# Message-passing layer of a GNN stack: ScalarE seeds four PSUM banks for each graph's first chunk, and TensorE adds onto the seed

## The chip, the core and the metric

The kernel runs on one core of one Trainium2 chip. The metric is the device time in microseconds of one execution, the median of three runs. The core has TensorE (PE, with a separate row for its weight loads, PEld), VectorE (DVE), ScalarE (ACT), GpSimd (POOL) and SyncE (SP). Each engine runs its own instruction list in order; they meet only at semaphores.

## The reference

Four GNN layers run over 128 graphs of 128 nodes with 64 features each; adj is 128x128x128. Only layer 0 is touched by the change. Cut to what matters:

```python
def _L0_gnn_ref(x, adj, W1, b1, W2, b2):          # x is relu(layernorm(x)) here
    F = x.shape[-1]
    mask = (adj > 0.0).astype(x.dtype)
    W1a, W1b = (W1[:F], W1[F:])
    xj_proj = x @ W1a
    diff = x[:, :, None, :] - x[:, None, :, :]
    h = jax.nn.relu(xj_proj[:, :, None, :] + diff @ W1b + b1)
    hm = jnp.einsum('bjkh,bjk->bjh', h, mask)
    deg = jnp.sum(mask, axis=-1)
    return hm @ W2 + deg[..., None] * b2
...
h = jnp.maximum(_layernorm(x, axis=-1), 0.0)
x = x + _L0_gnn_ref(h, adj, L0_gnn_W1, L0_gnn_b1, L0_gnn_W2, L0_gnn_b2)
```

For an edge from node j to node k the hidden vector is relu(A[j] - C[k]), 192 wide, where A = h(W1a + W1b) + b1 and C = h W1b. It is summed over the neighbours k of j. Layers 1 to 3 follow (three dense GCN products, a normalised layer, a tanh layer) and are the same before and after.

## The kernel before

The adjacency mask holds about 12% of the pairs, so layer 0 works on edges only. The neighbours of a node get ranks 0, 1, 2, ... and each rank is a slot. A **chunk** is up to seven slots of 128 nodes. For each slot a one-hot matrix picks, for every node j, row C[k] of the neighbour with that rank. Each graph has n - 1 **own chunks** of seven slots (n is counted on the chip; two own chunks in most graphs, three in some, 265 in all 128) and one **shared chunk** of five slots, in which nodes with many neighbours borrow rows of others.

The seven slots of an own chunk lie in four PSUM banks (table OWN): banks 0, 1 and 5 hold two slots each (384 columns), bank 6 one (192 columns). A and C are kept negated and split in two fp16 parts, ac_hi and ac_lo. `pe_chunk` fills one bank as follows: two matmuls with the identity as weights write -A (high, then low part) into all slots of the bank (line 524; the first has start=True), then each slot gets two matmuls with its one-hot matrix that add C (line 532). VectorE then takes the minimum with 0 and adds it into a sum in SBUF (line 722 for own chunks; lines 731 and 734 for the shared one), and that frees the bank (`s_free[k]`).

The work of **one graph b is one step** on every engine. Four graphs (q = 0 to 3) are a group; a loop iteration is two groups, eight graphs, and the loop is the hardware loop `Fori(1, NI - 1)` with 14 iterations, the first and the last two groups being written out. In a step the engines do, in program order:

- PE: at q = 0 the transposes of the next group's adjacency (lines 424, 427); the product that makes A and C of graph b + 2 (line 481, `pe_ac`); the own chunks in an inner loop; then `between`: the transposes of the summed result of graph b - 1 (lines 493 to 496), its update product for b - 2 (505, 506) and at each q a piece of the next group's ranking (433, 434, 442; 448; 454; 471 to 473); then the shared chunk.
- ACT: at q = 0 four copies of the transposes (571 to 576); at q = 1 seven copies of the ranks (588); two copies of `pe_ac`'s product, `ac` and `ac_hi` (622, 623); the start value of the sum for b + 1 (631, `act_init`); at q = 1 four normalisations (581); `act_sum` (637, 638); at q = 3 `act_host_ranks`, seven copies (603, 604, 607) that depend on PE's lines 471 to 473.
- DVE: the one-hot matrices of the next chunk (698), then the drains of the current one; between the own and the shared chunk the ranking arithmetic and the update of x (760).
- POOL: `ac_lo` (767), the host rows (775, 780), and the pairwise sums of the finished graph (789 to 793).

A ring of four chunks of one-hot matrices lies between DVE and PE. The result's transposes and `pe_ac`'s product use the same bank 2, so the transposes of graph b - 1 wait until `ac_hi` of graph b + 2 is copied:

```python
            if not (known(b) and b + 4 > B):
                pe.wait_ge(s_hi, b + 4)
```

(in `pe_transpose_sum`, called with b - 1.)

## Time and profile before

| what | value |
|---|---|
| median of 3 runs | 1949.1 us (1948.92 to 1950.03) |
| span of the profiled execution | 1947.1 us, 2.0 us less than the median |
| PE busy | 1728.4 us (89%) |
| PE weight loads | 1332.5 us (68%) |
| DVE busy | 1313.8 us (67%) |
| ACT busy | 974.0 us (50%) |
| POOL busy | 712.6 us (37%) |

The span runs from the first to the last instruction; the timed runs also hold what lies around it, here about 2.0 us. Layer 0 takes the span from about 40 to 1425 us. Busy time of PE is modelled for pipelined matmuls, so the distance between two starts says more about its pace than the length of one matmul.

### The profile page before, as it was taken

To read this page: it belongs to the slowest core of one execution; us is meant where nothing else is said; L and a number is where in the kernel's file an instruction comes from. 1 tells how busy PE (TensorE), PEld (TensorE's weight loads), DVE (VectorE), ACT (ScalarE), POOL (GpSimd) and SP (SyncE) were. 2 spreads that over 40 slices of the span, in tenths; PEclk is the share of its full clock that TensorE was granted. 3 is DMA by queue.
4 is the path that set the end of the run, shared out by engine and by line. 5 is a ranking of instruction groups with operands and counts; after the bars stand their busy time and mean duration, and the time that the engine had idled before them with its cause. 6 is when DMAs were issued, how large, how long until landed. Compare 5 with 4: busy or idle time off the path is not lost. (4 is left out here: it accounts for less than half of the span.)

```text
span 1947.1 us, 49676 instructions
## 1 busy us (share of the span) xinstructions
PE 1728.4 (89%) x13837; PEld 1332.5 (68%) x13838; DVE 1313.8 (67%) x3568; ACT 974.0 (50%) x2265; POOL 712.6 (37%) x866
## 2 busy tenths in 40 slices
PE   1899999999989999999999999999979998995399
PEld 0677676766767676676767676677769887970276
DVE  5687787767878776777878777688834444456633
ACT  2455444545544454554444455454245554744555
POOL 0444444544444454444545444454400000026400
PEclk9999999999999999999999999999989998997699
DMA  5000000000000000000000000000000000000012
GB/s 117 7 12 7 6 6 6 6 6 11 6 6 6 6 6 6 11 6 6 6 6 6 6 6 12 6 0 1 2 0 0 0 0 0 0 0 1 6 40 41
DMA packets 40222, 18.57 MB, mean 10 GB/s; under 512 B 18792, under 2 KB 40106, under 8 KB 40106
## 3 DMA queue, kind: packets, MB, share of 16 engines
q1 hardware_dynamic: 39574, 17.28, 3.7%
q14 instruction: 100, 0.82, 0.1%
q8 instruction: 16, 0.26, 0.1%
q10 hardware_dynamic: 532, 0.21, 0.1%
HBM read 13.29 MB, written 4.19 MB: 9 GB/s over the span
## 5 line engine op out<-in xcount | busy, mean ns | idle before, releaser
L532 PE MATMUL bank<-ac_hi,work 128*128 128x192 f16 x2495 | 535.6, 248 | 0.0
L532 PE MATMUL bank<-ac_lo,work 128*128 128x192 f16 x2495 | 535.5, 248 | 0.0
L722 DVE SCALAR_TENSOR_TENSOR acc<-bank,acc 128x384 f32<-128x384 f32 (+1 forms) x1060 | 467.9, 494 | 25.9 <-PE bank L532 20.0
L789 POOL TENSOR_TENSOR acc<-acc 128x384 f32<-128x384 f32 x256 | 267.5, 1065 | 593.4 <-DVE acc L734 593.4
L524 PE MATMUL bank<-ac_hi,ident 128*128 128x384 f16 (+1 forms) x1060 | 331.2, 312 | 81.2 <-DVE acc L722 58.6
L698 DVE TENSOR_SCALAR work<-work,slot_key 128x896 f16 (+2 forms) x393 | 264.8, 674 | 108.3 <-issue 105.6
L524 PE MATMUL bank<-ac_lo,ident 128*128 128x384 f16 (+1 forms) x1060 | 329.3, 311 | 0.0
L532 PEld LDWEIGHTS bank<-ac_lo,work 128*128 x2495 | 246.7, 99 | 70.7 <-issue 3.7
L532 PEld LDWEIGHTS bank<-ac_hi,work 128*128 x2495 | 246.4, 99 | 71.0 <-issue 3.7
L637 ACT ACTIVATE hmTa<-bank,unscale 128x128 f32<-128x128 f32 x128 | 47.1, 368 | 491.2 <-PE bank L496 491.2
L524 PEld LDWEIGHTS bank<-ac_hi,ident 128*128 128x128 f16 x1060 | 104.5, 99 | 153.6 <-DVE acc L722 85.5
L731 DVE TENSOR_SCALAR acc<-bank 128x384 f32<-128x384 f32 x256 | 132.1, 545 | 55.0 <-PE bank L532 54.1
L767 POOL TENSOR_TENSOR ac_lo<-ac,ac_hi 128x384 f16<-128x384 f32 x128 | 122.7, 959 | 68.1 <-ACT ac_hi L623 68.1
L622 ACT ACTIVATE ac<-bank 128x384 f32<-128x384 f32 x128 | 64.3, 502 | 135.9 <-PE bank L481 135.9
L588 ACT ACTIVATE work<-bank 128x512 f16<-128x512 f32 x224 | 113.1, 619 | 17.6 <-PE bank L434 17.6
L631 ACT ACTIVATE acc<-ac,neg_pad 128x768 f32<-128x768 f32 x128 | 121.8, 952 | 0.0
L1312 POOL MEMSET work<- 8x512 f32 x1 | 0.5, 515 | 316.1 <-POOLq L1104 316.1
L524 PE MATMUL bank<-ac_lo,host 128*128 128x384 f16 (+1 forms) x384 | 114.7, 299 | 0.0
L524 PE MATMUL bank<-ac_hi,host 128*128 128x384 f16 (+1 forms) x384 | 114.7, 299 | 0.0
L481 PE MATMUL bank<-wac,hT 65*128 65x384 f32 x256 | 109.4, 510 | 3.5 <-ACT ac_hi L623 3.5
L524 PEld LDWEIGHTS bank<-ac_lo,ident 128*128 128x128 f16 x1060 | 105.3, 99 | 9.3 <-issue 7.0
L968 ACT ACTIVATE hn<-x_all,nmr,rstd 128x64 f32 (+1 forms) x256 | 91.2, 430 | 27.9 <-PE bank L1122 26.5
(204 smaller groups left out, 3330.5 us busy)
## 6 DMA issues: line engine op xcount, KB each, us to landing
adj_in<-in_adj_dram SPq DMA_DIRECT2D x32, 256.0 KB, 2.9
out_dram<-acc SPq DMA_DIRECT2D x32, 128.0 KB, 2.0
l1w<-in_L_gnn_W_dram SPq DMA_DIRECT2D x2, 64.0 KB
l1b<-in_L_gnn_b_dram SPq DMA_DIRECT2D x2, 64.0 KB
x_all<-in_x_dram SPq DMA_DIRECT2D x4, 0.2 KB, 11.8
nm_in<-in_nodemask_dram ACTq DMA_DIRECT2D x1, 64.0 KB
w1a<-in_L_gnn_W_dram ACTq DMA_DIRECT2D x1, 48.0 KB
w1b<-in_L_gnn_W_dram ACTq DMA_DIRECT2D x1, 48.0 KB
```

Source lines behind the costliest of these rows:

```text
L481: nc.tensor.matmul(pAC[:, 0:2 * H], hT0[:, p, q * N:(q + 1) * N], wac[:, :], start=True, stop=True)\
L524: nc.tensor.matmul(ps[:, 0:slots * H].rearrange("p (t h) -> p t h", t=slots), node, part[:, q, 0:H].unsqueeze(1).broadcast_to([N, slots, H ...
L532: last = nc.tensor.matmul(ps[:, t * H:(t + 1) * H], hot, part[:, q, H:2 * H], start=False, stop=(e == 1 and t == slots - 1))
L588: last = nc.scalar.activation(rs[:, p, :, t, :], pA3[:, :].rearrange("p (q j) -> p q j", q=GS), ACT.Copy, bias=-float(t))
L622: nc.scalar.activation(ac32[:, q % 2, :], pAC[:, 0:2 * H], ACT.Copy)
L631: nc.scalar.activation(acc[:, q, :].rearrange("p (t h) -> p t h", t=4), ac32[:, q % 2, 0:H].unsqueeze(1).broadcast_to([N, 4, H]), ACT.Relu ...
L698: nc.vector.tensor_scalar(onehot[:, ds(at, slots * N)], ranks.rearrange("p t j -> p (t j)"), slot_key[:, ds(key, 1)], None, ALU.is_equal). ...
L722: nc.vector.scalar_tensor_tensor(out=sums, in0=bank[n_bank][:, 0:slots * H], scalar=0.0, in1=sums, op0=ALU.min, op1=ALU.add).then_inc(s_fr ...
L731: nc.vector.tensor_scalar(sums, ps, 0.0, None, ALU.min).then_inc(s_free[k], 1)
L767: nc.gpsimd.tensor_tensor(ac_lo[:, q, :], ac32[:, q % 2, :], ac_hi[:, q, :], ALU.subtract)\
L789: last = nc.gpsimd.tensor_tensor(t[:, 0:2 * H], t[:, 0:2 * H], t[:, 2 * H:4 * H], ALU.add)
L968: ins = nc.scalar.activation(hn[:, u, (q + 1) * F:(q + 2) * F], x[:, ds((b + q) * F, F)], ACT.Relu, bias=nmr[:, ds(b + q, 1)], scale=rstd[ ...
```

## The change

Each graph's first own chunk gets its -A from ScalarE. A new function `act_seed` writes the sum of both parts (ac32, in fp32) into the slots of the four banks with four ACTIVATE copies, in the order bank 5, 0, 1, 6; each waits for its own bank to be free and signals `s_seed[k]`. It stands at the very end of ACT's step b and seeds for graph b + 1. In PE's list the first own chunk is taken out of the inner loop; it waits for the seed of each bank and issues only the 14 one-hot matmuls, none with start=True. The eight identity matmuls of line 524 are gone from that chunk. The other own chunks and the shared chunk are as before. Once, at the start, four 512-column matmuls write all four banks with start=True (`pe_open_banks`), so that later matmuls add. `act_ac` gets one wait more. DVE and POOL keep their lists.

```diff
--- before.py
+++ after.py
@@ -398,6 +398,8 @@
         s_lo = sem("AC_low_part_made")
         s_acc0 = sem("sum_initialised")
         s_G = sem("onehot_chunk_made")
+        s_open = sem("slot_banks_written_once")
+        s_seed = [sem(f"bank{k}_seeded") for k, *_ in OWN]
         s_done = [sem(f"edges_in_bank{k}") for k, *_ in OWN]
         s_free = [sem(f"bank{k}_summed") for k, *_ in OWN]
         s_half = sem("neighbour_sums_paired")
@@ -511,7 +513,14 @@
             eng.reg_mul(pos, pos, CH)
             return eng.snap(pos, min_val=0, max_val=(RING - 1) * CH)
 
-        def pe_chunk(pe, q, banks, node, regs):
+        def pe_open_banks(pe):
+
+            pe.wait_ge(s_mask, 1)
+            for _, n_bank, *_ in OWN:
+                last = nc.tensor.matmul(bank[n_bank][:, :], ident16[:, :], mask[:, 0, :], start=True, stop=True)
+            last.then_inc(s_open, 1)
+
+        def pe_chunk(pe, q, banks, node, regs, seeded=None):
 
             cnt, prev, full_prev, pos = regs
             pe.reg_mov(prev, cnt)
@@ -519,25 +528,31 @@
             at = ring_place(pe, pos, prev)
             for k, n_bank, first, slots in banks:
                 ps = bank[n_bank]
-                pe.wait_ge(s_free[k], full_prev if k == 2 else prev)
-                for e, part in enumerate((ac_hi, ac_lo)):
-                    nc.tensor.matmul(ps[:, 0:slots * H].rearrange("p (t h) -> p t h", t=slots), node,
-                                     part[:, q, 0:H].unsqueeze(1).broadcast_to([N, slots, H]),
-                                     start=(e == 0), stop=False)
+                if seeded is not None:
+                    pe.wait_ge(s_seed[k], seeded + 1)
+                else:
+                    pe.wait_ge(s_free[k], full_prev if k == 2 else prev)
+                    for e, part in enumerate((ac_hi, ac_lo)):
+                        nc.tensor.matmul(ps[:, 0:slots * H].rearrange("p (t h) -> p t h", t=slots), node,
+                                         part[:, q, 0:H].unsqueeze(1).broadcast_to([N, slots, H]),
+                                         start=(e == 0), stop=False)
                 if k == 0:
                     pe.wait_ge(s_G, cnt)
                 for t in range(slots):
                     hot = onehot[:, ds(at + (first + t) * N, N)]
                     for e, part in enumerate((ac_hi, ac_lo)):
                         last = nc.tensor.matmul(ps[:, t * H:(t + 1) * H], hot, part[:, q, H:2 * H],
-                                                start=False, stop=(e == 1 and t == slots - 1))
+                                                start=False, stop=(e == 1 and t == slots - 1),
+                                                skip_group_check=seeded is not None)
                 last.then_inc(s_done[k], 1)
 
         def pe_slots(pe, b, g, u, q, regs, between):
             pe.wait_ge(s_lo, b + 1)
             pe.wait_ge(s_n, g + 1)
             n = pe.value_load(chunks[0:1, ds(b, 1)], min_val=MINC + 1, max_val=MAXC)
-            with pe.Fori(0, n - 1):
+            pe_chunk(pe, q, OWN, ident16[:, :], regs, b)
+            pe.reg_add(regs[2], regs[2], 1)
+            with pe.Fori(0, n - 2):
                 pe_chunk(pe, q, OWN, ident16[:, :], regs)
                 pe.reg_add(regs[2], regs[2], 1)
             between()
@@ -619,6 +634,7 @@
             if not (known(b) and b < 2):
                 act.wait_ge(s_lo, b - 1)
                 act.wait_ge(s_acc0, b - 1)
+                act.wait_ge(s_seed[3], b - 1)
             nc.scalar.activation(ac32[:, q % 2, :], pAC[:, 0:2 * H], ACT.Copy)
             nc.scalar.activation(ac_hi[:, q, :], pAC[:, 0:2 * H], ACT.Copy).then_inc(s_hi, 1)
 
@@ -631,6 +647,24 @@
             nc.scalar.activation(acc[:, q, :].rearrange("p (t h) -> p t h", t=4),
                                  ac32[:, q % 2, 0:H].unsqueeze(1).broadcast_to([N, 4, H]), ACT.Relu,
                                  scale=neg_pad[:, p, q:q + 1]).then_inc(s_acc0, 1)
+
+        def act_seed(act, b, q, regs):
+
+            total, full, n = regs
+            if known(b) and b == 0:
+                act.wait_ge(s_open, 1)
+            else:
+                act.reg_load(n, chunks[0:1, ds(b - 1, 1)])
+                act.reg_add(total, total, n)
+                act.reg_alu(n, n, 1, ALU.subtract)
+                act.reg_alu(n, n, MINC, ALU.max)
+                act.reg_add(full, full, n)
+            for k, n_bank, _, slots in (OWN[2], OWN[0], OWN[1], OWN[3]):
+                if not (known(b) and b == 0):
+                    act.wait_ge(s_free[k], full if k == 2 else total)
+                nc.scalar.activation(bank[n_bank][:, 0:slots * H].rearrange("p (t h) -> p t h", t=slots),
+                                     ac32[:, q % 2, 0:H].unsqueeze(1).broadcast_to([N, slots, H]), ACT.Copy)\
+                  .then_inc(s_seed[k], 1)
 
         def act_sum(act, b, p, q):
             act.wait_ge(s_T, b + 1)
@@ -807,6 +841,7 @@
                 pe.reg_mov(regs[2], 0)
                 pe_adj(pe, 0, 0, 0)
                 pe_rank(pe, 0, 0)
+                pe_open_banks(pe)
                 pe_degrees(pe, 0, 0)
                 pe_ac(pe, 0, 0, 0, 0)
                 pe_sum_rows(pe, 0)
@@ -849,6 +884,9 @@
 
             @block.scalar
             def _(act):
+                seeds = [act.alloc_register(f"act_{r}") for r in ("chunks", "own_chunks", "graph_chunks")]
+                act.reg_mov(seeds[0], 0)
+                act.reg_mov(seeds[1], 0)
                 act_h(act, 0)
                 act_adj(act, 0, 0)
                 act_h(act, 1)
@@ -857,6 +895,7 @@
                 act_ac(act, 0, 0)
                 act_ac(act, 1, 1)
                 act_init(act, 0, 0, 0, 0)
+                act_seed(act, 0, 0, seeds)
                 act_rank_nodes(act, 0)
                 act_host_ranks(act, 0, 0)
 
@@ -880,6 +919,8 @@
                         act_sum(act, b - 1, *group_of(b, g, u, q, 1)[1:])
                     if nxt is not None and q == 3:
                         act_host_ranks(act, nxt, p)
+                    if not (known(b) and b + 1 >= B):
+                        act_seed(act, b + 1, (q + 1) % GS, seeds)
 
                 all_iterations(act, step)
                 act_sum(act, B - 1, 1, 3)
```

**TensorE, from the product of line 481 to the first matmuls of a graph (before).** `bank0_summed` is DVE's release of bank 0:

```order
L481 MATMUL bank2<-wac,hT0 128x384 [waits AC_high_part_made,h_transpose_copied]
L539 TENSOR_LOAD chunks [waits slot_counts_ready,AC_low_part_made]
L539 ISA x2
L540 UNCONDITIONAL_BRANCH
L517 ISA
L510 REGISTER_ALU
L511 ISA
L524 MATMUL bank0<-ac_hi,ident16 128x384 [waits bank0_summed]
L524 MATMUL bank0<-ac_lo,ident16 128x384
L532 ISA [waits onehot_chunk_made]
L532 MATMUL bank0<-ac_hi,work 128x192
L532 MATMUL bank0<-ac_lo,work 128x192
```

The same place now (`bank0_seeded` is ScalarE's signal, line numbers are those of the changed kernel):

```order
L483 MATMUL bank2<-wac,hT0 128x384 [waits AC_high_part_made,h_transpose_copied]
L552 TENSOR_LOAD chunks [waits slot_counts_ready,AC_low_part_made]
L552 ISA x2
L526 ISA
L512 REGISTER_ALU
L513 ISA
L544 ISA [waits onehot_chunk_made,bank0_seeded]
L544 MATMUL bank0<-ac_hi,work 128x192
L544 MATMUL bank0<-ac_lo,work 128x192
L544 ISA
L544 MATMUL bank0<-ac_hi,work 128x192
L544 MATMUL bank0<-ac_lo,work 128x192
```

The pair of identity matmuls that waited for VectorE's release is gone, the register instruction ahead of the first one-hot matmul waits for the one-hot matrices and for the seed, and the entry of the inner loop (UNCONDITIONAL_BRANCH) has moved behind this chunk.

**ScalarE, from the end of a step with q = 3 to the next step (before).** `work` written from `ranks` are the slot ranks of `act_host_ranks`, `adjT_all` is the first copy of the next step:

```order
L603 ACTIVATE ranks2<-bank3 128x512 [waits host_ranks_made]
L604 ACTIVATE work<-bank4 128x512
L607 ACTIVATE work<-ranks2 128x4x128 [waits host_ranks_copied]
L607 ACTIVATE work<-ranks2 128x4x128 x4
L571 ACTIVATE adjT_all<-bank3 128x512 [waits adj_transposed]
```

Now:

```order
L618 ACTIVATE ranks2<-bank3 128x512 [waits host_ranks_made]
L619 ACTIVATE work<-bank4 128x512
L622 ACTIVATE work<-ranks2 128x4x128 [waits host_ranks_copied]
L622 ACTIVATE work<-ranks2 128x4x128 x4
L657 TENSOR_LOAD chunks
L658 ISA
L665 ACTIVATE bank5<-ac32 128x384 [waits bank2_summed]
L665 ACTIVATE bank0<-ac32 128x384 [waits bank0_summed]
L665 ACTIVATE bank1<-ac32 128x384 [waits bank1_summed]
L665 ACTIVATE bank6<-ac32 128x192 [waits bank3_summed]
L586 ACTIVATE adjT_all<-bank3 128x512 [waits adj_transposed]
```

The four writes into the banks, with a load of the chunk count ahead of them, now stand between the host ranks and the next step's first copy.

**ScalarE, from the end of a step with q = 0 to the next step (before).** `work<-bank` is the rank copy of line 588, which waits for TensorE's ranks:

```order
L631 ACTIVATE acc<-ac32,neg_pad 128x768 [waits neighbour_sum_ready,AC_high_part_made,slot_counts_ready]
L637 ACTIVATE hmTa<-bank2,unscale 128x128 [waits sum_transposed]
L638 ACTIVATE hmTb<-bank2,unscale 64x128
L588 ACTIVATE work<-bank3 128x4x128 [waits ranks_made]
L588 ACTIVATE work<-bank3 128x4x128 x6
L622 ACTIVATE ac32<-bank2 128x384 [waits sum_initialised,AC_low_part_made,AC_product_made]
```

Now:

```order
L671 ACTIVATE hmTa<-bank2,unscale 128x128 [waits sum_transposed]
L672 ACTIVATE hmTb<-bank2,unscale 64x128
L657 TENSOR_LOAD chunks
L658 ISA
L665 ACTIVATE bank5<-ac32 128x384 [waits bank2_summed]
L665 ACTIVATE bank0<-ac32 128x384 [waits bank0_summed]
L665 ACTIVATE bank1<-ac32 128x384 [waits bank1_summed]
L665 ACTIVATE bank6<-ac32 128x192 [waits bank3_summed]
L603 ACTIVATE work<-bank3 128x4x128 [waits ranks_made]
L603 ACTIVATE work<-bank3 128x4x128 x6
L638 ACTIVATE ac32<-bank2 128x384 [waits sum_initialised,bank3_seeded,AC_low_part_made,AC_product_made]
```

The seven rank copies stand behind four writes, each of which waits for VectorE to free a bank.

## Rows read from the trace of the kernel before

**Rows 1.** The page: busy time of each engine.

```profile
PE 1728.4 (89%) x13837; PEld 1332.5 (68%) x13838; DVE 1313.8 (67%) x3568; ACT 974.0 (50%) x2265; POOL 712.6 (37%) x866
```

**Rows 2.** The page, costliest groups: identity matmuls (first part), and the drains.

```profile
L722 DVE SCALAR_TENSOR_TENSOR acc<-bank,acc 128x384 f32<-128x384 f32 (+1 forms) x1060 | 467.9, 494 | 25.9 <-PE bank L532 20.0
...
L524 PE MATMUL bank<-ac_hi,ident 128*128 128x384 f16 (+1 forms) x1060 | 331.2, 312 | 81.2 <-DVE acc L722 58.6
```

**Rows 3.** Waits in 100:1380: total us, times, longest.

```profile
PE bank L524 <- DVE acc L722: 57.6, 73, 3.0
...
PE bank L524 <- DVE acc L731: 20.3, 30, 0.9
```

**Rows 4.** Timeline of PE at a q = 1 graph: start, us, line, operation.

```profile
618.00 0.33 PE L524 MATMUL bank<-ac_hi,ident 128*128 128x384 f16 x1
...
618.33 0.24 PE L532 MATMUL bank<-ac_hi,work 128*128 128x192 f16 x1
...
618.65 0.33 PE L524 MATMUL bank<-ac_hi,ident 128*128 128x384 f16 x1
...
620.66 0.34 PE L524 MATMUL bank<-ac_hi,ident 128*128 128x384 f16 x1 [0.20 <-DVE acc L722]
...
622.97 0.41 PE L493 MATMUL bank<-ident,hm 128*128 128x128 f32 x2
```

**Rows 5.** Timeline of DVE, same stretch.

```profile
617.25 1.00 DVE L731 TENSOR_SCALAR acc<-bank 128x384 f32<-128x384 f32 x2
618.36 0.36 DVE L734 SCALAR_TENSOR_TENSOR acc<-bank,acc 128x192 f32<-128x192 f32 x1
619.02 1.12 DVE L698 TENSOR_SCALAR work<-work,slot_key 128x896 f16 x1 [0.30 <-issue]
620.06 1.74 DVE L722 SCALAR_TENSOR_TENSOR acc<-bank,acc 128x384 f32<-128x384 f32 x4
```

**Rows 6.** Timeline of ACT, same stretch.

```profile
615.68 3.54 ACT L588 ACTIVATE work<-bank 128x512 f16<-128x512 f32 x7 [0.49 <-PE bank L434]
619.04 0.56 ACT L622 ACTIVATE ac<-bank 128x384 f32<-128x384 f32 x1
619.41 0.57 ACT L623 ACTIVATE ac_hi<-bank 128x384 f16<-128x384 f32 x1
```

**Rows 7.** Timeline of PE at the q = 0 graph before it.

```profile
608.72 0.33 PE L524 MATMUL bank<-ac_hi,ident 128*128 128x384 f16 x1
...
611.01 0.33 PE L524 MATMUL bank<-ac_hi,ident 128*128 128x384 f16 x1
...
613.31 0.41 PE L493 MATMUL bank<-ident,hm 128*128 128x128 f32 x2
```

**Rows 8.** Timeline of DVE, same stretch.

```profile
609.58 1.87 DVE L722 SCALAR_TENSOR_TENSOR acc<-bank,acc 128x384 f32<-128x384 f32 x3
```

**Rows 9.** Timeline of ACT, same stretch.

```profile
606.88 2.71 ACT L607 ACTIVATE work<-ranks 128x512 f16<-128x512 f16 x5
609.49 0.57 ACT L571 ACTIVATE adjT_all<-bank 128x512 f32 x1
...
611.97 0.47 ACT L623 ACTIVATE ac_hi<-bank 128x384 f16<-128x384 f32 x1
```

**Rows 10.** Timeline of DVE behind a loop turn (q = 0).

```profile
653.10 0.72 DVE L698 TENSOR_SCALAR work<-work,slot_key 128x896 f16 x1 [4.87 <-issue]
```

**Rows 11.** Timeline of PE behind the same loop turn.

```profile
654.35 0.34 PE L524 MATMUL bank<-ac_hi,ident 128*128 128x384 f16 x1 [3.02 <-DVE acc L722]
```

**Rows 12.** Windows behind two other loop turns; PEclk is the granted clock.

```profile
569.20:573.20 4.00, 3.93 (x22) 2.94 (x23) 2.71 (x8) 0.00 (x0) 0.00 (x0) 0.57 0.00 0
994.50:998.50 4.00, 3.99 (x35) 3.31 (x35) 3.55 (x9) 0.43 (x2) 0.00 (x0) 1.00 0.00 0
```

**Rows 13.** Timeline of PE at the first graph.

```profile
62.83 0.53 PE L524 MATMUL bank<-ac_hi,ident 128*128 128x384 f16 x1
...
65.84 0.33 PE L524 MATMUL bank<-ac_hi,ident 128*128 128x384 f16 x1
```

## The prediction

> **What bounds the kernel now.** I read the busy shares first: TensorE leads with 89%, VectorE and ScalarE have 67% and 50% [rows 1]. That invites the sum "TensorE is the bound, so what it no longer does is gained". The groups and the waits speak against it. Of all matmul groups only the identity matmuls are preceded by idle time to speak of, 81.2 us over the run, mostly behind VectorE's drains [rows 2]. Within layer 0 TensorE stood 73 times at a bank that line 722 had yet to drain and 30 times at one that line 731 had [rows 3]. So TensorE and VectorE hand each other the banks, and the place where they meet is the start of a graph. There I read the timelines of single graphs.
>
> At a q = 1 graph TensorE starts the first own chunk at 618.00 and could start the second one 2.30 us later, at 620.30, but starts at 620.66 [rows 4]: VectorE first ends the shared chunk of the graph before (618.72), builds the next one-hot matrices, and starts its drains at 620.06 [rows 5]; the first drained bank releases TensorE. I call this start C2. At q = 2 and q = 3 the two starts lie more than 2.30 us apart as well, in nearly all groups. At a q = 0 graph it is 2.29 us [rows 7]: there TensorE sets the pace. The 13 turns of the hardware loop are an exception: VectorE idles 4.87 us for nothing but its own issue [rows 10] and TensorE 3.02 us behind it [rows 11]. So C2 belongs to VectorE in every graph except the 18 q = 0 graphs that follow no loop turn (31 changes of group less 13 turns) and the very first.
>
> **What is removed.** Of a two-slot bank the identity pair takes 0.33 us from start to start, the four one-hot matmuls 0.32 us [rows 4]. Three such pairs and a half-size one are 1.15 us per graph, 147 us over 128 graphs. Where C2 waits for VectorE this buys no time: the one-hot matmuls of bank 0 were already done over 1 us ahead of the first drain (618.65 against 620.06), and VectorE's order, its one-hot work and its drains are not touched. The saved time becomes a longer wait before C2. The bank that TensorE needs is the cover; I cost these removals at zero in 109 of 128 graphs.
>
> The Trainium skill, in Perfetto Trace Analysis, section Identifying the Most-Contended Engine, says that busy matmul time is a poor measure of TensorE's headroom and points to the busy share of the weight loads instead. The trace agrees: that share is 68% [rows 1]. By it TensorE has room left; the 89% alone would promise the 147 us.
>
> **What is added on ScalarE.** Four writes per graph. No row shows a ScalarE write into PSUM. The nearest is the copy of 384 elements out of PSUM: 0.37 us from start to start [rows 6], 0.47 us long [rows 9]. Seven 512-column copies take 3.36 us to the next start, 0.48 each [rows 6], so 128 columns more are 0.11 us, and 192 columns should step on by 0.21 us. One graph's seeds then take 3 x 0.37 + 0.21 = 1.32 us. Bounds: 0.8 us (two copies and a bit, should writes to PSUM be much quicker) and 2.3 us (0.57 us each without overlap, the longest copy in rows 6). I take the nearest row, 1.32. ScalarE has the time, 128 x 1.32 = 169 us in a half-idle engine; what matters is where it stands.
>
> The skill's ScalarE: Activation LUTs, section What ACT_TABLE_LOAD costs, gives 186 ns plus 0.833 ns per element with 93 ns of overlap between neighbours, which makes an estimate of 0.41 us per step and 1.49 us per graph. By that estimate each late place below would cost 0.1 to 0.2 us more.
>
> **Place one: q = 3 to q = 0, 18 times.** The seeds stand behind the seven host-rank copies. ScalarE comes free at 609.49 [rows 9]. Bank 5 is seeded from there, bank 0 from 609.86 to 610.33. TensorE, ready at 608.72, starts bank 0 at about 610.43 instead of 609.05. Before, VectorE's drain began 0.53 us after that start (609.58, [rows 8]), so now 610.96; one drain (1.87 / 3 = 0.62) and 0.05 to notice give C2 = 611.63 against 611.01 [rows 7]. That is +0.6 us, where an early seed would have gained. The delay runs on: C2, transposes, shared chunk, VectorE's ranking work and the next drains follow one another. 18 x 0.6 = +10.8 us. Bounds 0.2 us (quick writes) and 1.5 us (1 us more of writes): 4 and 27 us. At the loop turns TensorE waits until 654.35 anyway [rows 11], and seeds done near 651 are covered: nothing.
>
> **Place two: q = 0 to q = 1, 31 times.** Here the seeds are not late for the matmuls, since VectorE drains only at 620.06. But they hold up what is queued behind them on ScalarE: seven rank copies and the `ac`/`ac_hi` pair. Bank 0 is free at about 617.77, bank 1 at 618.25, bank 6 at 618.72 [rows 5]. Seeds: 617.84, 618.31, 618.79; the rank copies can start at 619.0 instead of 615.68. `ac_hi` ended at 619.98 [rows 6]; it now ends 3.3 us later, at 623.3. The transposes of line 493 wait for it, since they use its bank, and would start at 622.97 [rows 4]; with some 0.1 us to notice that is +0.4 us. The next step's whole chain hangs on them. 31 x 0.4 = +12.4 us. Bounds 0 (ScalarE's copies 10% quicker) and 1.0 us (seeds one after the other without overlap): 0 and 31 us.
>
> At q = 0 itself `ac_hi` ended 0.87 us ahead of the transposes (612.44 against 613.31, [rows 7, 9]). It comes 1.32 us later and the transposes 0.6 us later: just in time, I count nothing; each further 0.1 us on ScalarE would cost 18 x 0.1. At q = 2 and q = 3 nothing long stands between the seeds and `ac_hi`, which comes at most 3 us later and had more than that to spare: nothing.
>
> **The rest.** The four opening matmuls lie at the start beside ScalarE's rank copies: nothing. The first graph's first chunk ran at the low clock, 3.01 us for 2.30 [rows 13], with its seeds long there: -1.5 us. Moving the inner loop's entry behind the first chunk costs nothing where TensorE waits for VectorE; at place one it has about 0.3 us to hide in.
>
> **The clock.** Behind a loop turn the granted clock is 0.57 in one window and 1.00 in another [rows 12]; of the 13 turns ten have such a dip. 0.57 over 4 us means 3.4 us at the lower of the two levels (1.2 instead of 2.4 GHz), 1.7 us of lost work. Before each turn's wait TensorE will now be less busy, so the three spared turns may dip too: up to +5 us, I take +2.5. The skill's TensorE: Matmul & The Clock Gate, section What's actually happening, says that activity is what releases the throttle; by that, sparser first chunks can only add dips.
>
> **Sum.** 10.8 + 12.4 - 1.5 + 2.5 = +24.2 us on a span of 1947.1 gives 1971.3; with the 2.0 us around it, which also separate the span from the median 1949.1, 1973.3 us: slower by 1.2%.
>
> **Rivals.**
> *TensorE bound after all.* If its work set the pace at most starts, some of the 147 us would come back. For it: 89% busy. Against it: the waits at C2. What it can really claim is the 18 q = 0 starts, where C2 could move from 611.01 to VectorE's first release near 610.2, 0.8 x 18 = 14 us, with place two free: about 1934. It needs ScalarE to seed in time there, against its order.
> *Everything covered.* ScalarE's writes are so quick or the delays so absorbed by waits of others that both places come to under 0.1 us: 1949. Against it: at both places the slack is smaller than the delay, by rows.
> *The clock falls in ordinary steps.* With 1.15 us less work around each start, TensorE is half idle for some 3 us. If that drops the clock behind the 18 late starts as it does behind loop turns, 18 x 1.7 = 31 us more: 2004. Against it: three turns with 3 us of idleness kept 1.00. This mechanism decides once it strikes more than a handful of starts.
> *ScalarE is slower at it than its copies.* At the upper bounds of both places, with register load and waits in its queue: +27 + 31 + about 18 x 0.5 for the transposes at q = 0: 2015.
>
> **Chances.** Forecast (1958 to 1990) 0.63, slower-ScalarE 0.10, clock 0.09, covered 0.10, TensorE bound 0.08. A run tells no change from one of 0.2%, about 4 us. Faster 0.09, same 0.10, slower 0.81. The range takes in the lower bounds of the two places and most of the two slower cases: 1953 to 2002; the forecast's own range is 1958 to 1990.
>
> **What would show it.** Right: TensorE's busy time lower by about 140 us at a longer span; a wait of 1.2 to 1.6 us at C2 for q = 1 to 3; a wait of ScalarE's seed at q = 0; a short idle time before the transposes at q = 1, ended by the copy of `ac_hi`. Wrong: C2 at q = 0 earlier than before relative to the shared chunk, seeds that take under 0.8 or over 2 us, or a granted clock below 1.00 away from the loop turns.

## The result and the profile after

| what | before | after |
|---|---|---|
| median of the runs | 1949.0 us (1948.5 to 1950.0, 4 runs) | 2006.4 us (2005.2 to 2006.8, 4 runs) |
| span of the profiled execution | 1947.1 us | 2003.6 us |
| mean granted clock | 0.966 | 0.943 |

The change makes the kernel 2.9% slower: the ratio is 1.0294, 95% interval 1.0279 to 1.0308. The forecast was 1973.3 us, its range 1953 to 2002; the sign was right and the size less than half of what was measured (24 of 57 us).

The page after, first its busy times and the clock in 40 slices, then three groups (columns: line, engine, operation, out<-in, shapes, count | busy us, mean ns | idle time before, releaser). L536 are the identity matmuls, L544 the one-hot ones, L665 the seeds:

```profile
PE 1655.7 (83%) x12817; PEld 1240.5 (62%) x12818; DVE 1313.2 (66%) x3568; ACT 1175.3 (59%) x2778; POOL 710.8 (35%) x866
...
PEclk9899998999999999989999999989989999998599
...
L544 PE MATMUL bank<-ac_hi,work 128*128 128x192 f16 x2495 | 532.3, 255 | 109.8 <-ACT bank L665 109.5
...
L665 ACT ACTIVATE bank<-ac 128x384 f32<-128x384 f32 (+1 forms) x512 | 218.4, 449 | 186.7 <-DVE acc L765 185.6
L536 PE MATMUL bank<-ac_hi,ident 128*128 128x384 f16 (+1 forms) x548 | 183.4, 335 | 94.7 <-DVE acc L756 94.1
```

TensorE has 73 us less work than in [rows 1], VectorE the same, ScalarE 201 us more, and the whole is 57 us longer. The idle time ahead of the identity matmuls was 81 us [rows 2] and is now 95 us, and a new one of 110 us stands ahead of the one-hot matmuls. The clock row shows an 8 in four slices of layer 0 where it held a 9 before.

The waits of 100 to 1430 us (columns: who waited for whom, us in total, times, longest) give the new pattern; they answer to [rows 3]:

```profile
ACT bank L665 <- DVE acc L765: 178.3, 90, 2.4
...
PE bank L544 <- ACT bank L665: 105.5, 120, 1.6
...
PE bank L536 <- DVE acc L756: 89.7, 104, 2.1
...
DVE acc L756 <- PE bank L544: 54.8, 67, 1.8
...
PE bank L495 <- ACT ac_hi L639: 6.7, 30, 0.3
```

TensorE waits for a seed 120 times, in nearly every graph of this stretch, and VectorE now waits 55 us for TensorE's first bank. The last row is place two of the prediction, 30 times.

**Place one (q = 0).** The graph of [rows 7 to 9] lies 23.52 us later here (its product for graph b + 2 starts at 631.59, before at 608.07). ScalarE:

```profile
630.39 2.71 ACT L622 ACTIVATE work<-ranks 128x512 f16<-128x512 f16 x5
633.00 1.55 ACT L665 ACTIVATE bank<-ac 128x384 f32<-128x384 f32 x4
634.50 0.58 ACT L586 ACTIVATE adjT_all<-bank 128x512 f32 x1
...
636.97 0.47 ACT L639 ACTIVATE ac_hi<-bank 128x384 f16<-128x384 f32 x1
```

TensorE and VectorE beside it:

```profile
634.03 0.25 PE L544 MATMUL bank<-ac_hi,work 128*128 128x192 f16 x1 [1.64 <-ACT bank L665]
...
635.20 0.25 PE L544 MATMUL bank<-ac_lo,work 128*128 128x192 f16 x1
635.49 0.33 PE L536 MATMUL bank<-ac_hi,ident 128*128 128x384 f16 x1
...
637.79 0.41 PE L495 MATMUL bank<-ident,hm 128*128 128x128 f32 x2
```

```profile
634.57 1.75 DVE L756 SCALAR_TENSOR_TENSOR acc<-bank,acc 128x384 f32<-128x384 f32 x4 [1.55 <-PE bank L544]
```

The seeds take 1.50 us to the next start (633.00 to 634.50), not 1.32. TensorE's first matmul starts 0.08 us from where it was forecast (634.03 - 23.52 = 610.51, forecast 610.43), but the second chunk starts at 635.49 - 23.52 = 611.97: 0.96 us later than the 611.01 of [rows 7], not 0.6. VectorE's drain is not what it waits for (there is no wait in that row). Its own way there is longer: 1.17 us from the first to the last of the 14 matmuls (13 steps of 0.08 us would be 1.05; the rest is the wait for the next seed), and then 0.29 us until the inner loop's first matmul starts, where the step within a chunk is 0.08. The weight load there stands behind 0.27 us of its own issue:

```profile
635.48 0.10 PEld L536 LDWEIGHTS bank<-ac_hi,ident 128*128 128x128 f16 x1 [0.27 <-issue]
```

**Place two (q = 1).** Shifted by 24.47 us against [rows 4 to 6] (product at 641.80, before at 617.33):

```profile
642.31 1.26 ACT L665 ACTIVATE bank<-ac 128x384 f32<-128x384 f32 x3 [2.19 <-DVE acc L765]
643.50 3.51 ACT L603 ACTIVATE work<-bank 128x512 f16<-128x512 f32 x7
...
647.21 0.57 ACT L639 ACTIVATE ac_hi<-bank 128x384 f16<-128x384 f32 x1
```

```profile
645.14 0.34 PE L536 MATMUL bank<-ac_hi,ident 128*128 128x384 f16 x1 [0.73 <-DVE acc L756]
...
647.83 0.49 PE L495 MATMUL bank<-ident,hm 128*128 128x128 f32 x2 [0.22 <-ACT ac_hi L639]
```

C2 stands where it did, within 0.02 us (645.14 - 24.47 = 620.67, against 620.66 in [rows 4]): here VectorE sets it, as forecast. `ac_hi` ends at 647.78, which is the forecast's 623.3 + 24.5, and the transposes wait for it and start 0.39 us later than in [rows 4].

**The clock.** The surprise stands at ordinary starts. Two q = 2 graphs with the same work, C2 to the transposes, as windows (columns: window, length, busy us and instructions of PE, PEld, DVE, ACT and POOL, granted clock, DMA share, GB/s):

```profile
475.70:479.70 4.00, 4.00 (x23) 2.94 (x24) 2.91 (x7) 0.75 (x1) 2.42 (x4) 0.57 0.00 0
566.70:570.70 4.00, 3.99 (x36) 3.31 (x37) 3.77 (x9) 1.19 (x3) 2.44 (x4) 1.00 0.00 0
```

In the first, TensorE gets mostly the lower of its levels (1.2 GHz) and does 23 matmuls where the second does 36. Its timeline ahead of the drop shows two waits in the 3.7 us before C2: 1.45 us for the seed, then the 14 one-hot matmuls of the first chunk, then 0.74 us at C2. The clock falls within the first identity matmuls:

```profile
473.49 0.25 PE L544 MATMUL bank<-ac_hi,work 128*128 128x192 f16 x1 [1.45 <-ACT bank L665]
...
474.71 0.25 PE L544 MATMUL bank<-ac_lo,work 128*128 128x192 f16 x1
475.69 0.45 PE L536 MATMUL bank<-ac_hi,ident 128*128 128x384 f16 x1 [0.74 <-DVE acc L756]
475.94 0.53 PE L536 MATMUL bank<-ac_lo,ident 128*128 128x384 f16 x1
...
479.67 0.41 PE L495 MATMUL bank<-ident,hm 128*128 128x128 f32 x2
```

From C2 to the transposes it took 3.98 us there and 2.31 us in the other graph. Before the change no ordinary start looked like this: between 100 and 1380 us there were ten low stretches, all at loop turns. After it there are 24 in the same window: at all 13 loop turns, ten of them twice as long as before, and at 11 ordinary starts (a twelfth lies behind 1380 us).

The two waits of a start, added, tell which starts are struck. Medians from the two timelines, loop turns left out:

| starts | waits before | waits after | starts with a drop after |
|---|---|---|---|
| q = 0 | 0.0 us | 1.7 us | 6 of 18 |
| q = 1 | 0.2 us | 1.0 us | none |
| q = 2 | 0.9 us | 1.9 us | 6 of 32 |
| q = 3 | 0.1 us | 0.9 us | none |

The drops fall where TensorE now idles most, though not at every such start.

**Where the 57 us went.** I took each graph's distances between three fixed points (start of the shared chunk of the graph before to C2, C2 to the transposes, transposes to the start of the shared chunk) from both timelines and subtracted:

| starts | number | forecast | measured | of this the clock |
|---|---|---|---|---|
| first graph | 1 | -1.5 | -2.1 | 0 |
| q = 0 behind no turn (place one) | 18 | +10.8 | +28.0 | 8.5 (6 graphs) |
| q = 1 (place two) | 32 | +12.4 | +14.4 | 0 |
| q = 2 | 32 | 0 | +9.3 | 9.3 (6 graphs) |
| q = 3 | 32 | 0 | -0.1 | 0 |
| loop turns | 13 | +2.5 | +8.6 | 13.6 (all 13) |
| sum | | +24.2 | +58.1 | 31.4 |

The clock's share of a graph is its excess over full-clock neighbours of the same q; at the loop turns it is what the way from C2 on has grown. In place one 19.5 us are left without the clock, 0.97 us in most graphs and 2.9 in the last of the 18. Behind layer 0 the two traces part by less than 2 us (58.1 against 56.5 us of span).

At the loop turns C2 itself comes 5.0 us earlier in sum, 0.4 each, and 4.7 of them are VectorE's. Before, GpSimd made `ac_lo` beside the first one-hot work behind the turn; now `ac_hi`, and with it `ac_lo`, comes later, and that work runs alone. The turn of [rows 10], before and then after:

```profile
652.66 0.91 POOL L767 TENSOR_TENSOR ac_lo<-ac,ac_hi 128x384 f16<-128x384 f32 x1 [1.09 <-ACT ac_hi L623]
```

```profile
677.86 0.45 DVE L732 TENSOR_SCALAR work<-work,slot_key 128x896 f16 x1 [4.68 <-issue]
...
679.09 0.91 POOL L801 TENSOR_TENSOR ac_lo<-ac,ac_hi 128x384 f16<-128x384 f32 x1 [2.58 <-ACT ac_hi L639]
```

The same instruction takes 0.45 us instead of 0.72 [rows 10]. In the trace of the kernel before, the 100 of these instructions that no GpSimd work overlaps take 0.43 to 0.46 us each; the 151 that GpSimd overlaps for more than half of their length take 0.99 us on average. This is read from the traces; no run isolates it.

### The profile page after: what moved, and what is told of

Read it like the earlier page. It is cut to its first block and busy times, and to the rows that moved or that the text cites. A ratio compares the mean times of both kernels' runs of the same rounds, so it can differ in the third digit from the quotient of the medians.

```text
span 2003.6 us, 48629 instructions
## 1 busy us (share of the span) xinstructions
PE 1655.7 (83%) x12817; PEld 1240.5 (62%) x12818; DVE 1313.2 (66%) x3568; ACT 1175.3 (59%) x2778; POOL 710.8 (35%) x866
## 5 line engine op out<-in xcount | busy, mean ns | idle before, releaser
L544 PE MATMUL bank<-ac_hi,work 128*128 128x192 f16 x2495 | 532.3, 255 | 109.8 <-ACT bank L665 109.5
L544 PE MATMUL bank<-ac_lo,work 128*128 128x192 f16 x2495 | 530.3, 254 | 0.0
L544 PEld LDWEIGHTS bank<-ac_hi,work 128*128 x2495 | 251.5, 101 | 265.2 <-issue 216.1
L665 ACT ACTIVATE bank<-ac 128x384 f32<-128x384 f32 (+1 forms) x512 | 218.4, 449 | 186.7 <-DVE acc L765 185.6
L544 PEld LDWEIGHTS bank<-ac_lo,work 128*128 x2495 | 252.8, 101 | 51.2 <-issue 10.8
L536 PE MATMUL bank<-ac_hi,ident 128*128 128x384 f16 (+1 forms) x548 | 183.4, 335 | 94.7 <-DVE acc L756 94.1
L536 PE MATMUL bank<-ac_lo,ident 128*128 128x384 f16 (+1 forms) x548 | 181.9, 332 | 0.0
L536 PEld LDWEIGHTS bank<-ac_hi,ident 128*128 128x128 f16 x548 | 56.8, 104 | 123.3 <-DVE acc L756 119.2
L536 PE MATMUL bank<-ac_lo,host 128*128 128x384 f16 (+1 forms) x384 | 114.8, 299 | 0.0
L536 PE MATMUL bank<-ac_hi,host 128*128 128x384 f16 (+1 forms) x384 | 114.8, 299 | 0.0
L809 POOL TENSOR_SCALAR host<-row_f,start 128x128 f16<-128x128 f32 x128 | 76.5, 612 | 85.6 <-DVE shift L723 85.6
```

What stands on the lines that cost most here:

```text
L536: nc.tensor.matmul(ps[:, 0:slots * H].rearrange("p (t h) -> p t h", t=slots), node, part[:, q, 0:H].unsqueeze(1).broadcast_to([N, slots, H ...
L544: last = nc.tensor.matmul(ps[:, t * H:(t + 1) * H], hot, part[:, q, H:2 * H], start=False, stop=(e == 1 and t == slots - 1), skip_group_ch ...
L665: nc.scalar.activation(bank[n_bank][:, 0:slots * H].rearrange("p (t h) -> p t h", t=slots), ac32[:, q % 2, 0:H].unsqueeze(1).broadcast_to( ...
```

## Experiments

All were timed beside runs of the kernel before on one chip: 1949.6 us (7 runs) for the first four, 1949.5 us (17 runs) for the others.

### The clock alone: the change with filler matmuls

```diff
+        def pe_fill(pe, b, count):
+            pe.wait_ge(s_x0, b - 2)
+            for _ in range(count):
+                nc.tensor.matmul(bank[7][:, 128:512]..., ident16[:, :], before16[:, :]..., start=True, stop=True)
...
                         pe_ac(pe, b + 2, *group_of(b, g, u, q, -2))
+                    fills = 7
+                    if fills and not (known(b) and b < 3):
+                        pe_fill(pe, b, fills)
```

Seven matmuls of 384 columns, whose result nobody reads, stand ahead of the first own chunk in every step from the fourth graph on.

> The changed kernel, and in every step from the fourth graph on TensorE issues seven matmuls of 384 columns into unused columns of bank 7, behind pe_ac and ahead of the first own chunk (1.15 us of work, about what the change took away; their result is never read). Theory A (of the 57 us, some 32 are the two late places and some 27 are new or longer stretches at the lower clock, because TensorE is too little busy around the start of a graph): the new stretches go, the places stay: about 1980 us (1975 to 1986), granted clock near 0.965. Theory B (the lower clock has another cause, or costs nothing and the time is lost elsewhere): 2004 to 2008. Theory C (TensorE's own work bounds the steps): slower than the changed kernel, up to 2006 + 147.

Measured: 1983.7 us (1982.0 to 1986.6, 4 runs), ratio 1.0174 (1.0157 to 1.0191): inside the expected range and 23 us less than the changed kernel. The same table reads, from the slowest of the four runs: q = 0 +19.0, q = 1 +14.3, q = 2 +0.1, loop turns +5.8. More work on TensorE made the kernel faster; q = 2 costs nothing any more, and the rest at q = 0 is place one without the clock. The two waits of a start, added, are back at 0.2, 0.8 and 0.1 us for q = 1 to 3 and 0.6 us for q = 0, and outside the loop turns no low stretch is left. So the clock's part is shown, and its cause is what TensorE does around the start. The turns kept a cost, of another kind: what follows C2 is 13.3 us shorter than before the change, but C2 comes 19.1 us later.

```profile
314.18 0.25 PE L544 MATMUL bank<-ac_lo,work 128*128 128x192 f16 x1
317.45 1.11 PE L426 MATMUL bank<-ident,adj_in 128*128 128x128 f32 x4 [3.03 <-issue]
```

The waits of this kernel have it 8 times in 13 turns:

```profile
PE bank L426 <- issue: 26.1, 8, 3.7
```

There TensorE itself stands still at the turn of the hardware loop, which it does neither before nor after the change, nor in any other run. Why is open.

### ScalarE's queue alone: four copies more, TensorE as before

```diff
@@ before
+            act.wait_ge(s_seed[3], b)
+            for k, n_bank, _, slots in (OWN[2], OWN[0], OWN[1], OWN[3]):
+                act.wait_ge(s_free[k], full if k == 2 else total)
+                nc.scalar.activation(spare[k], ac32[:, q % 2, 0:H]..., ACT.Copy).then_inc(s_seed[k], 1)
```

The kernel before, with the four copies at the seeds' place and with their waits (and the wait added to `act_ac`), but written to spare SBUF that nobody reads.

> The kernel before, and ScalarE makes the four copies of -A with the same waits at the same place, but into spare SBUF that nobody reads; TensorE does all its identity matmuls as before. Theory A (ScalarE's queue pays at q = 0 to 1 and at the transposes of q = 0, and the clock loss needs TensorE's missing work): 31 x 0.46 = 14 us and 18 x 0.5 to 0.7 = 11 us, clock as before: 1973 us (1968 to 1979). Rival (ScalarE's time is free, and the whole loss comes from TensorE waiting for seeds): 1949. Rival (the copies themselves upset the clock or VectorE): above 1990.

Measured: 1967.7 us (1962.5 to 1968.9, 4 runs), ratio 1.0087 (1.0068 to 1.0107), just under the expected 1968 to 1979. q = 1 costs 14.4 us, as much as in the changed kernel, so place two is ScalarE's order and has nothing to do with PSUM or TensorE. At q = 0 C2 does not move (0.0 us), but C2 to the transposes grows by 0.6 us each, 11.1 us. The waits name the cause:

```profile
PE bank L495 <- ACT ac_hi L626: 15.2, 46, 0.6
```

So the forecast's "just in time" for `ac_hi` at q = 0 was not just in time; in the changed kernel this cost lies hidden under the larger delay of C2 (there `ac_hi` ends at 637.44 and the transposes start at 637.79). The turns became 9.1 us shorter, which the expectation lacked: C2 comes 5.3 us earlier, mostly by VectorE's quicker one-hot work, as in the changed kernel (0.45 us at each turn, without GpSimd beside it), and the low stretches from 100 to 1380 us are eight instead of ten. The four copies take 1.49 us from start to start here too, from SBUF to SBUF, so the seeds' step is not a matter of PSUM. The mean clock of 100 to 1380 us is 0.99 as before: without sparser first chunks it does not drop more.

### Place two mended: four rank copies ahead of the seeds

```diff
-                            act_rank(act, nxt, p)
+                            act_rank(act, nxt, p, 4)
...
+                    if nxt is not None and q == 0:
+                        act_rank(act, nxt, p, 0, 4)
                     if not (known(b) and b + 1 >= B):
                         act_seed(act, b + 1, (q + 1) % GS, seeds)
```

> The changed kernel with one order changed on ScalarE: four of the seven rank copies stand ahead of the seeds of the q = 0 step, three behind them in the q = 1 step. Theory A: ac_hi is early again, the 0.46 us per q = 1 step go (14.5 us), nothing else moves but a stretch or two of low clock: 1992 us (1987 to 1997). Rival (the delay at q = 1 would be absorbed by the waits that follow): 2006. If seeds for q = 1 come late now, C2 moves at q = 1 and it is over 2006.

Measured: 1988.0 us (4 runs), ratio 1.0172 (1.0125 to 1.0219), inside the expected range but with wide scatter: 1972.2 us at a mean clock of 0.958 up to 1999.1 us at 0.941. The profiled run was the slowest. In it q = 1 went from +14.4 to +0.8 us, which settles place two; q = 2 rose to +17 us, all clock (13 graphs with a drop instead of six), so in this profile more than half of the gain was given back. With such scatter one profile does not show that the new order causes the additional drops.

### Place one mended: five host-rank copies behind the seeds

```diff
+                    if nxt is not None and q == 3:
+                        act_host_slot_ranks(act, nxt, p)
```

> The changed kernel with the other order changed on ScalarE: the five slot-rank copies of act_host_ranks stand behind the seeds of the q = 3 step instead of ahead of them. Theory A: the seeds are in time at q = 0, C2 comes 0.97 us earlier than now and up to 0.6 us earlier than in the kernel before at the 18 starts: 18 to 27 us, and fewer stretches of low clock at q = 0 (up to six of 1.4 us): 1978 us (1970 to 1989). Rival (slot ranks late for VectorE at the next one-hot work take it back): 1995 or more.

Measured: 1998.2 us (1991.8 to 2006.6, 4 runs), ratio 1.024 (1.0217 to 1.0264): the expectation of 1978 failed, and the rival's 1995 came by another cause than the one it named. In the profile, again of the slowest run, at q = 0 C2 comes 0.93 us earlier than before the change, the gain that the rival "TensorE bound" promised, and nothing of it remains:

```profile
631.47 0.34 PE L536 MATMUL bank<-ac_hi,ident 128*128 128x384 f16 x1
...
635.42 0.49 PE L495 MATMUL bank<-ident,hm 128*128 128x128 f32 x2 [1.49 <-ACT ac_hi L641]
```

The transposes now wait 1.49 us for `ac_hi`, which ScalarE reaches only behind seeds, host ranks, adjacency copies and `ac`. Up to C2 the sum over the 18 graphs is -16.8 us, from C2 to the transposes +26.7 us. The transposes of a typical q = 0 graph come 0.68 us later than before the change, as with ScalarE's copies alone. The order of seeds and slot ranks does not matter for that: both stand ahead of `ac_hi` either way. Other orders were not tried, such as `ac` and `ac_hi` ahead of the four adjacency copies; before the change their product was computed at about 608.9 and copied from 611.60 on. The rest of the time is clock again (q = 2: +21.7 us).

### Both orders mended

```diff
+                        act_rank(act, nxt, p, 0, 4)
...
+                        act_host_slot_ranks(act, nxt, p)
```

> The changed kernel with both orders changed on ScalarE (rank copies 4 and 3 around the seeds, slot-rank copies behind the seeds), nothing filled. Theory A: nothing lost at q = 1; at q = 0 C2 comes 0.9 us early but the transposes then wait for ac_hi, whose queue is 1.4 us longer with 0.87 us to spare: +0.55 us times 18 = 10 us; the clock takes 25 to 35 us: 1985 us (1975 to 1998), scattered. Rival (the early C2 is kept): 1950 to 1965.

Measured: 1971.4 us (1964.3 to 1989.5, 4 runs), ratio 1.0101 (1.0074 to 1.0128), the median 4 us under the expected range. The profiled run, again the slowest, has q = 0 at -16.8 and +26.8, q = 1 at +0.8, q = 2 at +23.2 (clock). The four runs line up by the clock: spans 1962.6, 1962.6, 1976.9 and 1987.9 us at mean clocks 0.956, 0.956, 0.947 and 0.943. The same program and data, so the spread of 25 us goes with the clock, and such drops are partly chance. Profiled was the slowest run alone, so the split of the faster ones is not known.

### No seed at q = 0, rank copies split, with and without filler

```diff
-            pe_chunk(pe, q, OWN, ident16[:, :], regs, b)
-            pe.reg_add(regs[2], regs[2], 1)
-            with pe.Fori(0, n - 2):
+            if q > 0:
+                pe_chunk(pe, q, OWN, ident16[:, :], regs, 3 * g + q - 1)
+                pe.reg_add(regs[2], regs[2], 1)
+            with pe.Fori(0, n - 1 if q == 0 else n - 2):
...
+            if q == 0:                               # in act_seed
+                return
...
+                    fills = 7 if q > 0 else 0        # in the first of the two kernels only
+                    if fills and not (known(b) and b < 3):
+                        pe_fill(pe, b, fills)
```

ScalarE seeds only the graphs of q = 1 to 3, so that both causes of place one are gone, and place two is mended as above.

> The changed kernel with all three suspected costs taken out: no seed for graphs with q = 0 (TensorE starts these itself, as in the kernel before), four rank copies ahead of the seeds of the q = 0 step and three behind, and seven idle matmuls of 384 columns into unused columns of bank 7 at q = 1 to 3 (their result is never read). Three quarters of ScalarE's seeds are still made and still used. Theory A (two late places and the clock are the whole loss, and the removed work was worth nothing): the time of the kernel before, 1949 us (1945 to 1954), clock near 0.966. Rival (something else in the seeds costs, such as the wait for them at q = 1 to 3): 1960 or more. Rival (the removed work is worth something once the late places are gone): under 1943.

> The same as the kernel with all three taken out, but without the idle matmuls. Theory A: what is above the kernel before is the clock alone: one stretch of about 1.5 us at some q = 2 graphs and longer stretches at loop turns: 1965 us (1957 to 1982), scattered from run to run, clock 0.945 to 0.958. Rival (idleness of TensorE at q = 1 to 3 does not touch the clock): 1949.

Measured: with filler 1949.2 us (1947.7 to 1950.5, 11 runs), ratio 0.9998 (0.9989 to 1.0007); without 1956.7 us (1954.0 to 1961.6, 6 runs), ratio 1.0045 (1.0032 to 1.0057). The first came as expected, the second just under its range. With both places and the clock taken care of, the whole loss is back, so nothing else in the seeds costs time. That kernel cannot show what the removed matmuls are worth, since the filler puts as much work in their place. The one without filler can: 96 graphs have 1.15 us less of TensorE's work each, and at q = 1 to 3 the way to C2 is the same to 0.2 us in sum over 32 graphs, since VectorE sets C2 there. In its profile q = 2 is +15.5 us, all of it low clock (ten graphs with a drop), while the turns are 7.5 us shorter than before, with five low stretches from 100 to 1380 us instead of ten. So the sparser starts do not simply add drops: here they came at q = 2 and fewer were left at the turns. Why is open.

### The kernel before with filler at the loop turns

```diff
@@ before
                         pe_ac(pe, b + 2, *group_of(b, g, u, q, -2))
+                    fills = 16 if (q == 0 and u == 0 and not known(b)) else 0
+                    if fills and not (known(b) and b < 3):
+                        pe_fill(pe, b, fills)
```

> The kernel before, with 16 idle matmuls of 384 columns (2.6 us) ahead of the first chunk of the first graph behind each loop turn, where TensorE stood idle for 3.0 us (their result is never read). Theory A (the low clock behind loop turns comes from that idle time, and VectorE's late one-hot work hides the filling): the ten stretches go, 10 x 1.65 = 16 us: 1933 us (1930 to 1938), clock 0.975 or more. Rival (low clock has another cause there): 1949. Rival (TensorE's longer instruction list stalls it at the turn, or the filling is on the path): 1950 or more.

Measured: 1935.2 us (1934.3 to 1936.7, 5 runs), ratio 0.9926 (0.9913 to 0.9939), as expected. It beats both kernels, with 224 matmuls more than before. At the turn of the first window of [rows 12] it reads:

```profile
563.67 2.76 PE L540 MATMUL bank<-before,ident 128*128 128x384 f16 x16
...
569.15 0.34 PE L524 MATMUL bank<-ac_hi,ident 128*128 128x384 f16 x1 [0.42 <-DVE acc L729]
```

The windows behind this turn and behind that of [rows 11]:

```profile
569.10:573.10 4.00, 3.95 (x34) 3.27 (x35) 3.60 (x9) 0.39 (x2) 0.00 (x0) 1.00 0.00 0
652.50:656.50 4.00, 3.96 (x35) 3.29 (x35) 3.58 (x9) 0.41 (x2) 0.00 (x0) 1.00 0.00 0
```

VectorE still idles at each turn (103.8 us of issue in its one-hot line over layer 0, as before), and TensorE still waits for it, but the filler takes up most of the wait: 0.42 us at C2 are left of 3.02. The clock holds at 1.00 in both windows, and no low stretch is left from 100 to 1380 us. The turns are 16.3 us shorter in sum. One graph is 2.6 us longer, the first of the hardware loop: the filler stands there too, behind no turn and with no wait to fill.

The mean granted clock of 100 to 1380 us beside it, one row for each of four kernels: before, after, the change with filler, and this one.

```profile
100.00:1380.00 1280.00, 1195.34 (x10035) 907.80 (x10035) 975.95 (x2623) 640.98 (x1412) 606.74 (x752) 0.99 0.02 6
```

```profile
100.00:1380.00 1280.00, 1080.40 (x8680) 787.48 (x8681) 932.89 (x2518) 793.77 (x1811) 576.48 (x719) 0.95 0.02 6
```

```profile
100.00:1380.00 1280.00, 1183.82 (x9621) 867.87 (x9619) 939.58 (x2544) 809.32 (x1841) 587.37 (x730) 0.98 0.03 7
```

```profile
100.00:1380.00 1280.00, 1229.38 (x10379) 929.98 (x10377) 984.47 (x2651) 645.25 (x1422) 612.33 (x760) 1.00 0.02 6
```

The clock is lowest where TensorE's busy time is, and highest where that is (1195, 1080, 1184 and 1229 of 1280 us).

## Why the prediction was right and wrong

**What bounds the kernel: right.** C2 at q = 1 to 3 stayed where VectorE puts it, and the 147 us of removed work bought nothing. The kernel with q = 0 left alone and without filler shows it most plainly: 96 graphs seeded, C2 where it was, and 7 us more by the clock.

**Place two: right in mechanism and size.** +12.4 forecast, +14.4 measured (0.38 us at the transposes and 0.07 behind them, where 0.4 was forecast), reproduced by ScalarE's copies alone and removed by splitting the rank copies.

**Place one: the mechanism right, the term too small.** 0.6 us was forecast, 0.97 measured in most of the 18 graphs, together 19.5 us without the clock instead of 10.8. Two steps failed. The seeds' length was taken from copies out of PSUM (0.37 us from start to start); it is 0.41. The estimate from the Trainium skill's ScalarE: Activation LUTs, section What ACT_TABLE_LOAD costs, which the prediction kept beside its sum, was 1.49 us per graph, and the row shows 1.50: it was nearer than my nearest row. And I let VectorE's first drain set C2, at 611.63, with "about 0.3 us to hide in" for the inner loop's entry. There was nothing to hide in: the 14 one-hot matmuls alone, 1.15 us from the forecast start of 610.43, end at 611.58. Seeds that release TensorE bank by bank cost it 0.2 us more (0.08 at the start, 0.1 between the banks), the entry another 0.2, and it reaches C2 at 611.97 by its own work. Both causes lie inside the upper bound of 1.5 us that was given.

**`ac_hi` at q = 0: right by luck.** "I count nothing" holds in the sum only because C2 was later than forecast; alone it costs 0.6 us per graph.

**The clock: the step that failed.** The term was +2.5 us and the trace has 31. The forecast looked only at the loop turns, and even there it counted up to three new dips, where the profile has 13.6 us more because the old ones became longer too; the rival that the clock falls at ordinary starts was written down, with 2004 us, and given a chance of 0.09. What I held against it was that three turns with 3 us of idleness kept 1.00 [rows 12]. That argument was upside down: ten of thirteen such turns did drop. The waits of a start rose from 0.9 us or less to 1.7 us (q = 0) and 1.9 us (q = 2), and these are the starts where the drops came. The rival had it nearly so, "TensorE is half idle for some 3 us": in the q = 2 graph above it waits 2.2 of the 3.7 us up to C2. The rival's time came near by a partly wrong working too: it put 31 us on the 18 late starts, and the drops were spread over six of these, six q = 2 starts and the turns. The kernels with filler win 23, 8 and 14 us with work that nobody reads, so it is TensorE's own activity that decides. Which of the sparse starts drop, and why fewer turns did in the kernel without filler, is open. The Trainium skill's TensorE: Matmul & The Clock Gate, section A second HAM failure mode: psum-queue depth-cycling, describes the like in another kernel: TensorE idles only briefly between groups of matmuls, and the clock still goes back and forth between its levels. The trace of the changed kernel agrees (waits of 1.45 and 0.74 us, then 0.57 in the window). The prediction had weighed another section of the same page of the Trainium skill.

**The signs to watch.** TensorE's busy time fell by 73 us and not by 140; the matmuls at the lower clock take part of it back, the rest I did not resolve. The wait at C2 was 0.73 us and not 1.2 to 1.6, since the first chunk itself starts later, behind its seeds. The wait for the seed at q = 0 and the short wait for `ac_hi` at q = 1 came as described. The sign named for a wrong forecast, a granted clock below 1.00 away from the turns, is what came.

**The sum by measured terms.** 19.5 (place one) + 14.4 (place two) - 2.1 (first graph) - 5.0 (C2 at the turns, mostly VectorE's quicker one-hot work, which the forecast did not have) + 31.4 (clock) = 58.2 us, and with the remainder behind layer 0 the 56.5 us of the spans.

## What to carry to other kernels

Work that is removed from an engine that waits anyway buys nothing, and what it leaves behind can cost: look at the granted clock in windows around the waits before thinning TensorE's work, and where some waits already drop it, expect more such drops. Put cheap matmuls that nobody reads into a known stall of TensorE; here 16 per loop turn gave 0.7% on the unchanged kernel. When work moves to another engine, price what is queued behind it there first: both places of this change were ScalarE's order, one was mended by splitting the rank copies, and the orders tried did not mend the other.

## What the runs showed that I had not expected

- The clock falls where TensorE is only partly idle: some 1.9 us of waiting in two pieces, around a sparse first chunk, stood ahead of the drop in six q = 2 graphs (0.57 in the window above), and the other 26 waited as long without one. A drop costs 1.3 to 1.7 us of a graph's chain.
- Such drops vary from run to run: one program spread over 25 us along with its mean clock (0.956 to 0.943), where the runs of the kernel before lie within 4 us (17 runs).
- A ScalarE copy of 384 fp32 elements from SBUF steps on by 0.41 us, into PSUM and into SBUF alike, against 0.37 us for a copy of the same size out of PSUM.
- VectorE's one-hot instruction of 128x896 takes 0.45 us alone and 0.99 us on average when GpSimd works beside it for more than half of it. A delay of GpSimd's `ac_lo` made it quicker at every loop turn.
- Entering an inner hardware loop costs TensorE 0.27 us of issue, some 0.2 us on the path at place one, and in one kernel the turn of the outer loop cost it 3.0 to 3.7 us in 8 of 13 turns. What decides the latter is open.
